# Moving the splits of the last output weight and of the adapter weights, and the making of the expert masks, forward in a one-core decoder layer

## The chip, the cores and the metric

The kernel runs on one core of one Trainium2 chip. The metric is the device time of one execution in microseconds (us): 538.18 us before the change, the median of 3 runs (537.94 to 539.28). Engines are PE (matrix products), DVE (vector), ACT (scalar), POOL (GpSimd) and SP, which here issues all the transfers.

## The reference, cut to what matters

`x` is 2 x 256 rows of 512. The layer does three things, each with a layer norm in front and a residual sum behind:

```
x += attn(ln(x))        32 heads of 128; q, k normed over all 4096 columns; out @ Wo + bo
x += fq(ln(x)) @ fq(ctx)            fake quantisation to 256 levels on both sides
x += base(ln(x)) + lora(ln(x))      15 router logits, softmax, top 8, expert_map -> 8 gates
```

In the last part `h = ln(x) @ A.T` gives 8 experts x 16 columns, each expert's columns are multiplied by its gate, and the product with `B` is added. The gate of an expert is the sum of the kept router probabilities whose entry of `expert_map` is that expert.

## The kernel before, in words

Matrix products are made with a split: each f32 operand is written as a rounded part ("hi", fp32r) and the remainder ("lo", operand minus hi), and a product is hi*hi + hi*lo + lo*hi, three matmuls. ACT makes the hi parts (a copy), DVE or POOL the lo parts (a subtraction whose inputs are both in SBUF, for weights, k and q).

The first 190 us or so project k and q for all 32 heads. Then come 16 pairs of heads, `pair(p)` on every engine, p = 0 to 15; each pair has four slots j = 0 to 3, one for each head and batch row. Pairs 1 to 10 stand in a hardware loop, pairs 11 to 15 are written out, so that `peeled(p, first, end)` can put something into one of them alone. Pair 15 (`last=True`) has no v projection for a following pair and no fourth v or output weight.

The order on each engine is written by hand. In a slot PE does: scores of the next slot (`scores`, L529 to L542), transposes of this slot's probabilities (L544), a tile of the next pair's v (L552), output projection of the head before (`project_out`, L569), and probabilities times v (`probs_v`, L590). At even slots nothing new is needed for the scores; at odd slots `scores` begins with a new head, and waits for its k and q splits, `pe.wait_ge(kq_lo, 2 * h + 2)` at L533. These k_lo and q_lo are made by POOL at the start of the even slot (`split_kq_lo`, L951), from k_hi and q_hi of ACT (L748, L751). There is one buffer each. In every slot POOL also makes the lo part of one weight (`chunk_lo`, L942: w_lo at even slots, wo_lo at odd ones), behind ACT's hi part (L745, L827).

DVE in a slot: o_lo of the head before (L1200, even slots), the row maximum nmax of the scores (L1178), nbias = nmax * rq_t (L1180, a tiny product of two SBUF tensors for which ACT's exponentials wait, L762), pt_lo (L1247), the reciprocal rinv and two scalings of the probabilities by it (L1186, L1188, L1189; PE's transposes wait for these), and v_lo at odd slots (L1194).

The last output weight (head 31) has buffers of its own: it is loaded at L383 behind the loads of pair 14, its hi part is made by ACT in slot 0 of pair 15 (L820), its lo part by POOL in slot 2 (L986). The adapter weights ra (A and the router, 576 columns) and bm (B, 512 columns) are loaded at L372 and L373; ACT makes their hi parts behind pair 15 (L839, L841), POOL the lo parts in slot 3 of pair 15 (`split_low_rank`, L969). The expert masks (`mark_experts`, L960: a cast of the map and 8 comparisons of 128x15) are made by POOL in the quantisation stage behind the pairs (L1008). DVE reads them at L1386.

Of the kernel before, what the change touches and what calls it, by code (L numbers as in the profile page):

```python
# [19 lines left out]
F32 = mybir.dt.float32  # L20
# [3 lines left out]
ALU = mybir.AluOpType  # L24
# [3 lines left out]
P = 128  # L28
B, S, D = 2, 256, 512
# [4 lines left out]
NH, DH = 32, 128  # L34
NP = NH // 2
# [13 lines left out]
def decoder_layer(nc, x, ctx_t, wk, wq, wv, wo, bk, bq, bv, bo, gk, gq, qscal, ra_w, base_b, router_b, bm_w,  # L49
                  expert_map, out):  # L50
    st = ExitStack()
    with st:
# [20 lines left out]
        def here(name, shape, dt, at=None):  # L73
            return place(name, shape, dt, at)[0]
# [56 lines left out]
        KS = T * 4  # L131
# [39 lines left out]
        bm_lo = here("bm_lo", [P, D], F32R, q_at + 21 * KS)  # L171
        wo_last_hi = here("wo_last_hi", [P, D], F32R, q_at + 22 * KS)
        wo_last_lo = here("wo_last_lo", [P, D], F32R, q_at + 23 * KS)
        wo_last_f = here("wo_last_f", [P, D], F32, q_at + 26 * KS)
        o_last_hi = here("o_last_hi", [P, T], F32R, q_at + 24 * KS)
        o_last_lo = here("o_last_lo", [P, T], F32R, q_at + 25 * KS)
        hwt_hi = here("hwt_hi", [P, NT, P], F32R, qh_at)
# [106 lines left out]
        def peeled(n, first, end):  # L284

            return isinstance(n, int) and first <= n < end
# [22 lines left out]
        @block.sync  # L309
        def _(sp):  # L310
            for t in range(NT):
                sp.dma_start(xin[:, t, :], x[t]).then_inc(x_landed[t], 16)
            for r in range(4):
                sp.dma_start(raw[:, r, :], wk[r]).then_inc(w_landed[r], 16)
            for dst, src in ((bk_c, bk), (bq_c, bq), (bv_c, bv), (g_c, gk), (gq_c, gq)):
                sp.dma_start(dst[:], src).then_inc(const_landed, 16)

            def load_heads(w, i, before):

                for r in range(4):  # L320
                    sp.wait_ge(w_lo_dve, before + 4 * i + r - 3)
                    sp.dma_start(raw[:, r, :], w[bass.ds(4 * i + r, 1)].rearrange("a p n -> (a p) n")
                                 ).then_inc(w_landed[r], 16)

            sp.dma_start(qs_b[:], qscal.partition_broadcast(P)).then_inc(qs_landed, 16)
            for i in range(1, NH // 4):
                load_heads(wk, i, 0)
                if i <= NT:
                    g = slice(2 * (i - 1), 2 * i)
                    sp.dma_start(ctx_f[:, g, :], ctx_t[:, g, :]).then_inc(ctx_landed[i - 1], 16)  # L330
                if i == NT:
                    sp.dma_start(bo_b[:], bo.partition_broadcast(P)).then_inc(x_bo_landed, 16)
                    for t in range(NT):
                        sp.dma_start(xb[:, t, :], x[t]).then_inc(x_bo_landed, 16)
            sp.wait_ge(ctx_quantised, B * NC // 2)
            sp.dma_start(ctx_kept, ctx_k[:]).then_inc(ctx_kept_out, 16)
            with sp.Fori(0, NH // 4) as i:
                load_heads(wq, i, NH)

            def load_wv(pair, c, n):  # L340
                sp.dma_start(raw[:, n, :], wv[bass.ds(2 * pair + c, 1)].rearrange("a p n -> (a p) n")
                             ).then_inc(w_landed[n], 16)

            def load_wo(h):
                sp.dma_start(raw[:, 1, :], wo[bass.ds(h, 1)].rearrange("a p n -> (a p) n")
                             ).then_inc(w_landed[1], 16)

            for n in range(4):

                sp.wait_ge(w_lo_dve, U1 - 3 + n if n < 2 else U1 + n - 1)  # L350
                load_wv(n // 2, n % 2, n % 2)

            def pair_loads(p):
                for j in range(3 if peeled(p, NP - 1, NP) else 4):
                    if peeled(p, 0, 1) and j < 2:
                        sp.wait_ge(w_lo_dve, U1 + 3 + j)
                    else:
                        sp.wait_ge(w_lo_pool, 4 * p + j - 1)
                    if j % 2:
                        load_wo(2 * p + j // 2)  # L360
                    else:
                        load_wv(p + 2, j // 2, 0)

            pair_loads(0)
            with sp.Fori(1, 8) as p:
                pair_loads(p)

            pair_loads(8)
            pair_loads(9)
            sp.wait_ge(scores_ready, 2 * 18)  # L370
            pair_loads(10)
            sp.dma_start(ra_f[:], ra_w).then_inc(ra_landed, 16)  # L372
            sp.dma_start(bm_f[:], bm_w).then_inc(bm_landed, 16)  # L373
            sp.dma_start(bb_b[:], base_b.partition_broadcast(P)).then_inc(base_b_landed, 16)
            sp.dma_start(rb_b[:], router_b.partition_broadcast(P)).then_inc(router_b_landed, 16)
            sp.dma_start(em_i[:], expert_map.partition_broadcast(P)).then_inc(map_landed, 16)
            pair_loads(11)
            sp.wait_ge(scores_ready, 2 * 22)
            sp.wait_ge(ctx_kept_out, 16)
            sp.dma_start(ctx_q[:], ctx_kept).then_inc(ctx_back, 16)  # L380
            for p in range(12, NP - 1):
                pair_loads(p)
            sp.dma_start(wo_last_f[:], wo[NH - 1]).then_inc(wo_last_landed, 16)  # L383
            pair_loads(NP - 1)
            for t in range(NT):
                sp.wait_ge(out_done, t + 1)
                sp.dma_start(out[t], xn[:, t, :]).then_inc(stored, 16)
            sp.wait_ge(stored, 16 * NT)
# [297 lines left out]
        def _(act):  # L686
# [55 lines left out]
            def pair_weights_hi(n, buf, half_, landed):  # L742

                act.wait_ge(w_landed[n], 16 * (NH // 2 + landed))
                act.copy(w_hi[:, buf, half_ * 512:(half_ + 1) * 512], raw[:, n, :]).then_inc(w_hi_done, 1)  # L745
# [48 lines left out]
            def pair(p, par, last=False):  # L794
                for j in range(4):
# [19 lines left out]
                        exps(h + b, 1 - b)  # L815
                    if b == 1 and not last:
                        v_half_hi(p + 1, j // 2, 1 - par)
                    if last and j == 0:
                        act.wait_ge(wo_last_landed, 16)
                        act.copy(wo_last_hi[:], wo_last_f[:]).then_inc(wo_last_hi_done, 1)  # L820
                    if last and j == 3:
                        pass
                    elif b == 1:
                        act.wait_ge(w_landed[1], 16 * (NH // 2 + 3 + 2 * p + j // 2))
                        if not peeled(h, 0, 1):
                            act.wait_ge(wo_used, h)
                        act.copy(wo_hi[:], raw[:, 1, :]).then_inc(w_hi_done, 1)  # L827
                    else:
                        pair_weights_hi(0, par, j // 2, 3 + 2 * p + j // 2)

            pair(0, 0)
            with act.Fori(0, (NP - 6) // 2) as i:
# [2 lines left out]
            for p in range(NP - 5, NP - 1):  # L835
                pair(p, p % 2)
            pair(NP - 1, 1, last=True)
            act.wait_ge(ra_landed, 16)
            act.copy(ra_hi[:], ra_f[:]).then_inc(rab_hi_done, 1)  # L839
            act.wait_ge(bm_landed, 16)  # L840
            act.copy(bm_hi[:], bm_f[:]).then_inc(rab_hi_done, 1)  # L841
            last_out_hi(1)


# [60 lines left out]
        def _(pool):  # L905
# [41 lines left out]
            def pair_chunk_lo(buf, half_, slot, n):  # L947
                cols = slice(half_ * 512, (half_ + 1) * 512)
                chunk_lo(w_lo[:, buf, cols], w_hi[:, buf, cols], slot, n)
# [16 lines left out]
                    ins = pool.tensor_scalar(onehot[:, e, :], emf[:], float(e), None, ALU.is_equal)  # L966
                ins.then_inc(experts_marked, 1)

            def split_low_rank():  # L969

                pool.wait_ge(rab_hi_done, 1)
                pool.tensor_tensor(ra_lo[:], ra_f[:], ra_hi[:], ALU.subtract).then_inc(rab_lo_done, 1)
                pool.wait_ge(rab_hi_done, 2)
                pool.tensor_tensor(bm_lo[:], bm_f[:], bm_hi[:], ALU.subtract).then_inc(rab_lo_done, 1)

            def pair(p, par, last=False):
                for j in range(4):
                    h = 2 * p + j // 2
                    if j % 2 == 0 and not (last and j == 2):
                        split_kq_lo(h + 1)  # L980
                    if last and j == 3:
                        split_low_rank()
                        break
                    if last and j == 2:
                        pool.wait_ge(wo_last_hi_done, 1)
                        pool.tensor_tensor(wo_last_lo[:], wo_last_f[:], wo_last_hi[:], ALU.subtract  # L986
                                           ).then_inc(wo_last_done, 1)
                    if j % 2:
                        chunk_lo(wo_lo[:], wo_hi[:], 1, 4 + 4 * p + j)
                    else:  # L990
                        pair_chunk_lo(par, j // 2, 0, 4 + 4 * p + j)
                    if peeled(p, NP - 5, NP - 4) and j == 0:
                        pool.memset(ones_b[:], 1.0).then_inc(ones_b_made, 1)

# [9 lines left out]
            for g in range(2):  # L1004
                pool.wait_ge(var_ready, g + 1)
                pool.tensor_tensor(rstd[:, 2 * g:2 * g + 2], vare[:, 2 * g:2 * g + 2], mhalf[:, 0:2], ALU.pow
                                   ).then_inc(rstd_ready, 1)
            mark_experts()  # L1008
            for t in range(NT):
                pool.wait_ge(var_ready, 3 + t)  # L1010
                pool.tensor_tensor(rstd[:, t:t + 1], vare[:, t:t + 1], mhalf[:, 0:1], ALU.pow).then_inc(rstd_ready, 1)
# [448 lines left out]
```

## Time and profile before

| | us |
|---|---|
| median of 3 runs | 538.18 (537.94 to 539.28) |
| the profiled execution's own time | 540.05 |
| its span, first to last instruction | 537.7 |
| PE busy in the span | 523.5 |
| DVE, ACT, POOL busy | 331.1, 355.9, 271.6 |

All times in views are from the start of the span. The engines' busy times overlap. The granted TensorE clock is 1.00 all through. In the profiled execution the projections end near 190 us, pair 13 is the stretch from 441.35 to 460.10, pair 14 that to 478.87, pair 15 that to 496.30; the quantised product, the experts and the output follow to 537.7. Where a view lists an instruction, the first number is its start and the second its duration.

### The profile page before, as it was taken

How to read it: one execution, taken by the hardware profiler on the slowest of the kernel's cores; microseconds unless marked ns; L12 is line 12 of the kernel's file. 1: busy time of each engine (PE TensorE's matmuls, PEld its weight loads, DVE VectorE, ACT ScalarE, POOL GpSimd, SP SyncE). 2: the span in 40 equal slices, each digit the busy share in tenths (PEclk: the TensorE clock that was granted, in tenths of full speed). 3: DMA queues.
4: the chain of work that ended last, by engine and by line, in shares of the span. 5: the costliest groups of instructions: out<-in, count | busy, mean ns of one | idle time of the engine just before them, and what ended most of it. 6: DMA issues, size and time to landing. Idle time of an engine off the chain costs nothing.

```text
span 537.7 us, 9702 instructions
## 1 busy us (share of the span) xinstructions
PE 523.5 (97%) x3198; PEld 462.0 (86%) x3198; DVE 331.1 (62%) x695; ACT 355.9 (66%) x745; POOL 271.6 (51%) x229
## 2 busy tenths in 40 slices
PE   6999999999999999999999999999999999999887
PEld 6888888888888888999999999999999999986475
DVE  6254444266666677666666666666666666676755
ACT  3566666556666767777777677767767776775740
POOL 3344444365454445554646455464646556465340
PEclk9999999999999999999999999999999999999999
DMA  5344635323332221112122111211142311220002
GB/s 182 126 139 134 230 96 174 89 89 98 94 100 83 74 81 55 47 57 60 59 59 59 57 43 56 59 59 59 59 121 62 126 50 60 60 78 21 2 0 79
DMA packets 23350, 43.41 MB, mean 81 GB/s; under 512 B 3616, under 2 KB 3616, under 8 KB 23072
## 3 DMA queue, kind: packets, MB, share of 16 engines
q1 hardware_dynamic: 23328, 43.13, 26.3%
q8 instruction: 12, 0.20, 0.2%
q14 instruction: 10, 0.08, 0.0%
HBM read 41.03 MB, written 2.10 MB: 80 GB/s over the span
## 4 chain that ended last, share of the span: by engine, by line
PE 90%; DVE 5%; ACT 2%; DMA 1%; issue 1%; POOL 1%; SPq 0%; DVEq 0%
PE p_t L483 5%; PE p_v L562 5%; PE p_v L564 5%; PE p_o L483 5%; PE p_t L484 5%; PE p_o L484 5%; PE p_v L563 5%; PE p_o L486 5%; PE p_t L486 5%; PE acc L581 5%; PE acc L582 5%; PE acc L583 5%; PE p_t L548 5%; PE p_o L600 3%; PE p_o L602 3%; PE p_o L601 3%
## 5 line engine op out<-in xcount | busy, mean ns | idle before, releaser
L1078 DVE TENSOR_TENSOR w_lo<-raw,w_hi 128x512 fp32r<-128x512 f32 x64 | 44.2, 690 | 78.0 <-ACT w_hi L693 78.0
L945 POOL TENSOR_TENSOR wo_lo<-raw,wo_hi 128x512 fp32r<-128x512 f32 x31 | 40.1, 1294 | 100.4 <-ACT wo_hi L827 100.4
L693 ACT CAST w_hi<-raw 128x512 fp32r<-128x512 f32 x64 | 39.9, 623 | 67.5 <-PE p_t L486 30.3
L762 ACT ACTIVATE probs<-p_s,nbias,rq_t 128x256 f32<-128x256 f32 x128 | 71.3, 562 | 19.1 <-DVE nbias L1180 19.1
L562 PE MATMUL p_v<-w_hi,xnt_hi 128*128 128x256 f32 x256 | 77.2, 301 | 0.0
L564 PE MATMUL p_v<-w_hi,xnt_lo 128*128 128x256 f32 x256 | 72.3, 282 | 0.0
L563 PE MATMUL p_v<-w_lo,xnt_hi 128*128 128x256 f32 x256 | 72.2, 282 | 0.0
L927 POOL TENSOR_TENSOR acc_k<-acc_k,square 128x512 f32<-128x512 f32 x32 | 41.7, 1304 | 53.3 <-ACT square L708 53.3
L927 POOL TENSOR_TENSOR acc_q<-acc_q,square 128x512 f32<-128x512 f32 x32 | 43.5, 1361 | 40.2 <-ACT square L708 39.9
L811 ACT CAST pt_hi<-p_t 128x512 fp32r<-128x512 f32 x64 | 37.4, 584 | 38.8 <-PE p_t L548 38.8
L945 POOL TENSOR_TENSOR w_lo<-raw,w_hi 128x512 fp32r<-128x512 f32 x32 | 44.9, 1403 | 20.5 <-ACT w_hi L745 20.5
L1178 DVE TENSOR_REDUCE nmax<-p_s 128x2 f32<-128x512 f32 x64 | 43.9, 686 | 14.9 <-PE p_s L541 14.0
L483 PE MATMUL p_t<-xnt_hi,w_hi 128*128 128x512 f32 x128 | 50.4, 394 | 0.7 <-ACT xnt_hi L717 0.7
L581 PE MATMUL acc<-wo_hi,o_hi 128*128 128x512 f32 x124 | 49.4, 398 | 1.0 <-POOL wo_lo L945 0.6
L484 PE MATMUL p_t<-xnt_hi,w_lo 128*128 128x512 f32 x128 | 49.8, 389 | 0.0
L483 PE MATMUL p_o<-xnt_hi,w_hi 128*128 128x512 f32 x128 | 49.8, 389 | 0.0
L484 PE MATMUL p_o<-xnt_hi,w_lo 128*128 128x512 f32 x128 | 49.8, 389 | 0.0
L486 PE MATMUL p_o<-xnt_lo,w_hi 128*128 128x512 f32 x128 | 49.8, 389 | 0.0
L562 PEld LDWEIGHTS p_v<-w_hi,xnt_hi 128*128 128x128 f32 x256 | 48.8, 190 | 0.3 <-issue 0.2
L582 PE MATMUL acc<-wo_hi,o_lo 128*128 128x512 f32 x124 | 49.0, 395 | 0.0
L563 PEld LDWEIGHTS p_v<-w_lo,xnt_hi 128*128 128x128 f32 x256 | 48.9, 191 | 0.0
L564 PEld LDWEIGHTS p_v<-w_hi,xnt_lo 128*128 128x128 f32 x256 | 48.7, 190 | 0.0
(263 smaller groups left out, 1483.7 us busy)
## 6 DMA issues: line engine op xcount, KB each, us to landing
raw<-in_wv SPq DMA_DIRECT2D x36, 256.0 KB, 2.6
raw<-in_wk SPq DMA_DIRECT2D x32, 256.0 KB, 2.6
raw<-in_wq SPq DMA_DIRECT2D x32, 256.0 KB, 2.6
raw<-in_wo SPq DMA_DIRECT2D x31, 256.0 KB, 2.6
ctx_f<-in_ctx SPq DMA_DIRECT2D x4, 512.0 KB, 3.6
xin<-in_x SPq DMA_DIRECT2D x4, 256.0 KB, 3.5
xb<-in_x SPq DMA_DIRECT2D x4, 256.0 KB, 6.0
ctx_kept<-ctx_k SPq DMA_DIRECT2D x1, 1024.0 KB, 5.0
```

The lines of the kernel that those rows point to most:

```text
L483: pe.matmul(p_flat[2 + n], hi[:, c, :], xnt_hi[:, c, :], start=(c == 0), stop=False)
L484: pe.matmul(p_flat[2 + n], lo[:, c, :], xnt_hi[:, c, :], start=False, stop=False)
L486: mm = pe.matmul(p_flat[2 + n], hi[:, c, :], xnt_lo[:, c, :], start=False, stop=(c == NC - 1))
L562: pe.matmul(p_v[:, t % 2, :], xnt_hi[:, c, tt], hi[:, c, :], start=(c == 0), stop=False)
L563: pe.matmul(p_v[:, t % 2, :], xnt_hi[:, c, tt], lo[:, c, :], start=False, stop=False)
L564: mm = pe.matmul(p_v[:, t % 2, :], xnt_lo[:, c, tt], hi[:, c, :], start=False, stop=(c == NC - 1))
L581: pe.matmul(acc[t][:], oh[:, tt], wh[:], start=False, stop=False, skip_group_check=True)
L582: pe.matmul(acc[t][:], ol[:, tt], wh[:], start=False, stop=False, skip_group_check=True)
L762: act.activation(probs[:, b, a, :], p_s[:, a, :], ACT.Exp, bias=nbias[:, b, a:a + 1], scale=rq_t[:, 2 * b + a:2 * b + a + 1], accum_out=rs ...
L927: pool.tensor_tensor(sums[:], sums[:], square[:, r % 2, :], ALU.add).then_inc(summed, 1)
L945: pool.tensor_tensor(dst, raw[:, slot, :], hi, ALU.subtract).then_inc(w_lo_pool, 1)
L1078: dve.tensor_tensor(w_lo[:, n, 0:NC * DH], raw[:, r, :], w_hi[:, n, 0:NC * DH], ALU.subtract).then_inc(w_lo_dve, 1)
```

## The change

Four things move, nothing is computed otherwise:

- The transfer of the last output weight is issued by SP right behind that of bm, before pair 11's loads (it stood behind pair 14's); its buffer lies over head 4 of k_all, which is dead by then.
- ACT makes ra_hi in slot 0 of pair 13, bm_hi in slot 1 and wo_last_hi in slot 2, each behind the hi part of that slot's weight.
- POOL makes ra_lo, bm_lo and wo_last_lo in the same slots, each behind the lo part of that slot's weight.
- POOL makes the expert masks at the end of slot 3 of pair 14.

```
-        wo_last_f = here("wo_last_f", [P, D], F32, q_at + 26 * KS)
+        wo_last_f = here("wo_last_f", [P, D], F32, k_at + 4 * KS)
 # SP
             sp.dma_start(bm_f[:], bm_w).then_inc(bm_landed, 16)
+            sp.dma_start(wo_last_f[:], wo[NH - 1]).then_inc(wo_last_landed, 16)
...
                 pair_loads(p)
-            sp.dma_start(wo_last_f[:], wo[NH - 1]).then_inc(wo_last_landed, 16)
             pair_loads(NP - 1)
 # ACT, in pair()
-                    if last and j == 0:
-                        act.wait_ge(wo_last_landed, 16)
-                        act.copy(wo_last_hi[:], wo_last_f[:]).then_inc(wo_last_hi_done, 1)
...
+                    if peeled(p, NP - 3, NP - 2):
+                        if j == 0:
+                            act.wait_ge(ra_landed, 16)
+                            act.copy(ra_hi[:], ra_f[:]).then_inc(rab_hi_done, 1)
+                        elif j == 1:
+                            act.wait_ge(bm_landed, 16)
+                            act.copy(bm_hi[:], bm_f[:]).then_inc(rab_hi_done, 1)
+                        elif j == 2:
+                            act.wait_ge(wo_last_landed, 16)
+                            act.copy(wo_last_hi[:], wo_last_f[:]).then_inc(wo_last_hi_done, 1)
...
             pair(NP - 1, 1, last=True)
-            act.wait_ge(ra_landed, 16)
-            act.copy(ra_hi[:], ra_f[:]).then_inc(rab_hi_done, 1)
-            act.wait_ge(bm_landed, 16)
-            act.copy(bm_hi[:], bm_f[:]).then_inc(rab_hi_done, 1)
 # POOL; last_weights_lo(j) holds the three subtractions, one for each j = 0, 1, 2
                     if last and j == 3:
-                        split_low_rank()
                         break
-                    if last and j == 2:
-                        pool.wait_ge(wo_last_hi_done, 1)
-                        pool.tensor_tensor(wo_last_lo[:], wo_last_f[:], wo_last_hi[:], ALU.subtract
-                                           ).then_inc(wo_last_done, 1)
                     if j % 2:
                         chunk_lo(wo_lo[:], wo_hi[:], 1, 4 + 4 * p + j)
                     else:
                         pair_chunk_lo(par, j // 2, 0, 4 + 4 * p + j)
+                    if peeled(p, NP - 3, NP - 2):
+                        last_weights_lo(j)
+                    if peeled(p, NP - 2, NP - 1) and j == 3:
+                        mark_experts()
...
-            mark_experts()
             for t in range(NT):
                 pool.wait_ge(var_ready, 3 + t)
```

## Rows read from the trace of the kernel before

**Rows 1.** The page's engine line: busy us, share of the span, instructions.
```profile
PE 523.5 (97%) x3198; PEld 462.0 (86%) x3198; DVE 331.1 (62%) x695; ACT 355.9 (66%) x745; POOL 271.6 (51%) x229
```

**Rows 2.** Windows, pairs 13 and 15: length; busy PE, PEld, DVE, ACT, POOL; clock; DMA.
```profile
441.35:460.10 18.75, 18.75 (x138) 17.72 (x137) 12.56 (x28) 13.62 (x33) 10.49 (x8) 1.00 0.19 57
...
478.87:496.30 17.43, 15.42 (x90) 11.97 (x88) 10.97 (x23) 12.47 (x29) 11.45 (x9) 1.00 0.09 31
```

**Rows 3.** Timeline of PE in slot 3 of pair 13: start, duration, instruction.
```profile
455.43 0.28 PE L539 MATMUL p_s<-k_hi,q_hi 128*128 128x256 f32 x1
...
456.15 0.60 PE L548 MATMUL p_t<-ident,probs 128*128 128x128 f32 x4
```

**Rows 4.** Timeline of POOL in slots 0 to 2 of pair 13; idle before, its releaser in brackets.
```profile
446.11 1.41 POOL L945 TENSOR_TENSOR w_lo<-raw,w_hi 128x512 fp32r<-128x512 f32 x1 [0.58 <-ACT w_hi L745]
450.97 1.29 POOL L945 TENSOR_TENSOR wo_lo<-raw,wo_hi 128x512 fp32r<-128x512 f32 x1 [3.46 <-ACT wo_hi L827]
452.35 1.30 POOL L953 TENSOR_TENSOR k_lo<-k_all,k_hi 128x512 fp32r<-128x512 f32 x1
453.61 1.30 POOL L955 TENSOR_TENSOR q_lo<-q_all,q_hi 128x512 fp32r<-128x512 f32 x1
455.49 1.41 POOL L945 TENSOR_TENSOR w_lo<-raw,w_hi 128x512 fp32r<-128x512 f32 x1 [0.58 <-ACT w_hi L745]
```

**Rows 5.** Timeline of DVE in pair 13.
```profile
447.70 0.16 DVE L1180 TENSOR_TENSOR nbias<-nmax,rq_t 128x2 f32<-128x2 f32 x1
...
455.14 0.36 DVE L1188 TENSOR_SCALAR probs<-probs,rinv 128x256 f32<-128x256 f32 x1
455.40 0.35 DVE L1189 TENSOR_SCALAR probs<-probs,rinv 128x256 f32<-128x256 f32 x1
```

**Rows 6.** Timeline of ACT in pair 13, slots 0 and 1.
```profile
447.40 0.59 ACT L811 CAST pt_hi<-p_t 128x512 fp32r<-128x512 f32 x1 [1.38 <-PE p_t L548]
...
450.27 0.62 ACT L827 CAST wo_hi<-raw 128x512 fp32r<-128x512 f32 x1 [0.70 <-PE acc L583]
```

**Rows 7.** The low part of ra on POOL: duration ns min/median/max, starts.
```profile
L972 POOL TENSOR_TENSOR ra_lo<-ra_f,ra_hi x1: 1427/1427/1427, 494.0 to 494.0; 128x576 fp32r<-128x576 f32 x1
```

**Rows 8.** DVE's scaling L1163 near 110 us, all four instances: ns min/median/max.
```profile
L1163 DVE TENSOR_SCALAR diag<-ident,rk_t x4: 276/793/1316, 109.6 to 112.3; 128x128 f32<-128x128 f32 x4
```

**Rows 9.** Timeline of POOL beside them.
```profile
109.57 2.72 POOL L927 TENSOR_TENSOR acc_q<-acc_q,square 128x512 f32<-128x512 f32 x2
```

**Rows 10.** Timeline of POOL, the expert masks.
```profile
501.99 0.21 POOL L963 CAST emf<-em_i 128x15 f32<-128x15 int32 x1
502.29 2.24 POOL L966 TENSOR_SCALAR onehot<-emf 128x15 f32<-128x15 f32 x8
```

**Rows 11.** Timeline of POOL across the start of pair 15 and its slot 2.
```profile
479.11 1.28 POOL L945 TENSOR_TENSOR wo_lo<-raw,wo_hi 128x512 fp32r<-128x512 f32 x1 [3.46 <-ACT wo_hi L827]
480.49 1.30 POOL L953 TENSOR_TENSOR k_lo<-k_all,k_hi 128x512 fp32r<-128x512 f32 x1
481.74 1.28 POOL L955 TENSOR_TENSOR q_lo<-q_all,q_hi 128x512 fp32r<-128x512 f32 x1
...
488.63 1.29 POOL L986 TENSOR_TENSOR wo_last_lo<-wo_last_f,wo_last_hi 128x512 fp32r<-128x512 f32 x1
```

**Rows 12.** Timeline of PE in pair 15: the scores of head 31, and the last transposes.
```profile
483.33 0.28 PE L539 MATMUL p_s<-k_hi,q_hi 128*128 128x256 f32 x1
...
492.08 0.66 PE L548 MATMUL p_t<-ident,probs 128*128 128x128 f32 x4 [0.51 <-DVE probs L1189]
```

**Rows 13.** Timeline of DVE in pair 15: nbias in slots 0 and 2.
```profile
481.18 0.62 DVE L1180 TENSOR_TENSOR nbias<-nmax,rq_t 128x2 f32<-128x2 f32 x1
...
489.24 0.70 DVE L1180 TENSOR_TENSOR nbias<-nmax,rq_t 128x2 f32<-128x2 f32 x1
```

**Rows 14.** Timeline of SP's transfers after the three small ones.
```profile
398.28 0.43 SPq L376 DMA_DIRECT2D em_i<-in_em  x1
400.81 0.33 SPq L341 DMA_DIRECT2D raw<-in_wv  x1
```

More of the change, by code:

```diff
@@ L967, in mark_experts, with last_weights_lo @@
                 ins.then_inc(experts_marked, 1)
[L969 to L974, printed above, removed]
+            def last_weights_lo(j):
+                if j == 0:
+                    pool.wait_ge(rab_hi_done, 1)
+                    pool.tensor_tensor(ra_lo[:], ra_f[:], ra_hi[:], ALU.subtract).then_inc(rab_lo_done, 1)
+                elif j == 1:
+                    pool.wait_ge(rab_hi_done, 2)
+                    pool.tensor_tensor(bm_lo[:], bm_f[:], bm_hi[:], ALU.subtract).then_inc(rab_lo_done, 1)
+                elif j == 2:
+                    pool.wait_ge(wo_last_hi_done, 1)
+                    pool.tensor_tensor(wo_last_lo[:], wo_last_f[:], wo_last_hi[:], ALU.subtract
+                                       ).then_inc(wo_last_done, 1)
             def pair(p, par, last=False):
```

## Prediction, made before the changed kernel ran

> **What bounds the kernel now.** I read the page's engine line first: PE is busy 97% of the span [rows 1]. Then the windows by pair: in pair 13 PE is busy 18.75 of 18.75 us while POOL has 10.49 us of work and ACT 13.62; in pair 15 PE has 15.42 of 17.43 us and the others are no fuller [rows 2]. So up to the end of pair 14 whatever makes PE wait is paid in full, since PE has no later idle time there to give it back, and work taken off ACT, DVE or POOL gains nothing. In pair 15 and behind it the end is set by chains through all engines. The third view is the timeline of each engine in pairs 13 and 15, which shows what has room. Times below are those of before, with delays added.
>
> POOL sits idle 3.46 us ahead of wo_lo, but almost nothing lies between wo_lo, k_lo and q_lo, and q_lo ends at 453.61 + 1.30 = 454.91 [rows 4], when PE wants to begin the scores of the new head at 455.43 [rows 3]. That is 0.52 us of room. In pair 15 q_lo ends at 481.74 + 1.28 = 483.02 and the scores begin at 483.33 [rows 11, 12]: 0.31 us. The question is what is put in front of these two.
>
> **A lock between DVE and POOL.** nbias is a product of 128x2. It takes 0.16 us in an odd slot, when POOL is idle [rows 5], and 0.70 us at 489.24 [rows 13], and that one ends at 489.94, just when POOL's wo_last_lo ends (488.63 + 1.29 = 489.92) [rows 11]. The one at 481.18 ends at 481.80, with k_lo (481.79). So a small DVE operation with both inputs in SBUF waits for POOL's whole subtraction. The DVE scaling L1163, one SBUF tensor by a column of scalars like L1188 and L1189, takes 276 ns at its shortest and 1316 at its longest, with a median of 793 [rows 8], while POOL runs two additions back to back in 2.72 us [rows 9]. Two short and two long ones fit only if the first waited for the first addition, POOL's second addition then got in ahead of DVE's second scaling, and that waited once more. I take that as the rule for L1188 and L1189: under back-to-back POOL work each of the two can wait for one POOL operation.
>
> The Trainium skill ("SBUF — State Buffer", "Who interferes with whom") says of the same thing that a DVE instruction with two SBUF inputs contends with a GpSimd instruction that reads SBUF, and that a tensor_scalar contends if it is in a 2-port mode; the loser blocks for the whole instruction. The nbias rows agree with its first half. Were L1188 and L1189 not in such a mode, the sum would lose the handover term below.
>
> **SP's transfer.** One issue more near 397 us. The last small one starts at 398.28 and the next weight load at 400.81, waiting for POOL [rows 14], so 0.43 us more is hidden in 2.1 us; if it weren't, that load would start 0.4 us late and still be long ahead of its use. The removed issue at pair 14 gains nothing. Cost 0 (bounds 0 and 0.4).
>
> **ACT in pair 13.** ra_hi goes into 1.38 us of idle before pt_hi [rows 6]: free. wo_last_hi, in slot 2, goes into the like gap: free. bm_hi (a copy of the size of wo_hi, 0.62 [rows 6]) stands behind wo_hi with o_hi, k_hi, q_hi, pt_hi queued behind it; they slip by its 0.6 us, but POOL, busy with bm_lo, takes k_hi and q_hi later still, and o_lo, which follows o_hi, stays ahead of PE's product. So nothing is added to what follows; if that cover failed, 0.2 us.
>
> **POOL in pair 13, slot 0.** ra_lo (1.43) [rows 7] starts when w_lo ends, 446.11 + 1.41 = 447.52, and ends at 448.95. nbias starts at 447.70 and has both inputs in SBUF [rows 5], so it ends at 448.95 and not at 447.86: 1.09 us late. The exponentials follow it. PE needs the result two microseconds later, so PE loses nothing here, but ACT is late: of the 1.1 us, wo_hi has 0.70 of idle ahead of it [rows 6] and starts 0.35 late.
>
> **POOL in pair 13, slots 1 and 2.** wo_lo starts at 450.97 + 0.35 = 451.32. Back to back, one POOL subtraction starts 1.25 us after the other (453.61 less 452.35 [rows 4]). So bm_lo starts at 452.57, k_lo at 453.82, q_lo at 455.07, and q_lo ends at 456.37. With 0.1 us for the signal PE starts the scores at 456.5 and not at 455.43 [rows 3]: 1.05 us late. The bounds of this part: 1.25 less 0.52 = 0.7 (bm_lo alone, no delay from slot 0), and 1.2.
>
> Then the handover. L1188 starts at 455.14, L1189 at 455.40, both just after q_lo's end in the trace before [rows 4, 5]. Now they come while q_lo runs to 456.37. L1188 waits for it; w_lo is queued on POOL by then, gets in next, and runs for 1.25 us to about 457.7; L1189 ends near 457.9. PE's transposes need it. They started at 456.15 [rows 3] and start now at 457.9: 1.8 us late. This holds the 1.05 within it, so the handover adds 0.75. The bounds of the handover are 0 and 0.9. From then on all engines run 1.8 us late in the same order, and wo_last_lo, put behind w_lo, has POOL's idle 3.46 us as cover; nbias of slot 3 waits for it until 459.0, but the exponentials behind it also stand behind pt_hi, and that behind the transposes of 457.9, so it costs nothing more.
>
> **POOL at the end of pair 14.** The masks take from 501.99 to 504.53, 2.54 us for nine instructions [rows 10]. They start behind wo_lo at 479.11 + 1.28 = 480.39 (again in the clock of before). k_lo started at 480.49 [rows 11], so k_lo and q_lo start 2.4 us later and q_lo ends at about 485.4. In the same stretch L1188 and L1189 of slot 0 fall on k_lo and q_lo and hand the lock over twice, 0.1 each: 485.6. PE starts the scores of head 31 at 485.75 in place of 483.33 [rows 12]: 2.4 us. Bounds: 2.1 (no handover) and 2.7.
>
> What comes back of it: nbias in slot 2 took 0.70 us because of wo_last_lo [rows 11, 13], which is gone from there, and nothing else of POOL runs then, since wo_lo is ahead of it and w_lo waits for ACT's copy behind the exponentials. 0.70 less 0.16 is 0.54, and it lies on the chain nbias, exponentials, scalings, last transposes at 492.08 [rows 12]. The 0.46 us of slot 0 (0.62 less 0.16) is swallowed by the wait for the scores, and slot 1 follows PE. So pair 15 costs 2.4 less 0.54, some 1.85 us (bounds 1.3, if more of the nbias relief counts, and 2.3, if none does).
>
> **Behind the pairs.** ra_hi, bm_hi, ra_lo and bm_lo leave the end of pair 15, and the masks the quantisation stage. The last products there start when PE is ready, not when these are; POOL's next work, rstd, waits for DVE's variances. I cost their removal at 0 (bounds 0 and a gain of 0.1).
>
> **Sum.** 1.8 + 1.85 = 3.65 us later. Against the profiled execution's own time that is 540.05 + 3.65 = 543.7 us (span 541.3). That execution is 1.87 us above the median of the runs, so for a median I add the 3.65 to 538.18: 541.8 us. By the skill's condition failing (no 2-port mode for L1188 and L1189), it would be 541.0.
>
> **Rivals.**
>
> No handover: the scalings are not held by POOL, or DVE's second goes ahead of w_lo. Pair 13 costs 1.05 and pair 15 1.65: 2.7 us, 540.9. For it: L1188 and L1189 overlap with a running POOL operation nowhere in this trace, so the reading by L1163 is by likeness only. Against it: 1316 ns of L1163.
>
> The masks are cheaper: POOL takes them in without the 2.5 us, as the eight tiny comparisons overlap with the waits around them. Then pair 15 gains its 0.54, pair 13 costs 1.8: 1.3 us slower, 539.5, no change that can be told. Against it: k_lo follows wo_lo after 0.10 us; there is no wait to hide in.
>
> Not slower: the lock's relief decides. If q_lo of the new head reaches PE in time in both places (POOL's spans being rough, the 0.52 and 0.31 us of room would have to be 1.3 and 2.5), then the three nbias of pair 15 shorten, by 0.46 and 0.54 and that of slot 1 by as much at most, 1.5 us in all, and the time is 536.7 to 538.2. It decides from the point where the masks and bm_lo cost less than the room ahead of the scores. Against it: the POOL rows of pairs 13 and 15 agree with the ends of nbias to 0.02 us, so they are not rough by 0.8.
>
> Worse: the lag in pair 13 spills over. v_lo of slot 1 and o_lo of slot 2 come out of the delay of 1.1 us with some tenths left; if PE has to wait for one of them, or a further scaling loses the lock for 1.25 us, it is 3.65 and about 1: 542.8.
>
> **Chances.** Forecast 0.53, no handover 0.23, cheap masks 0.09, not slower 0.08, worse 0.07. About 0.3% (1.6 us) is what a measurement of this kernel can tell from no change. Slower by more than that: 0.83, the forecast, no handover and worse. Within: 0.13, the cheap masks and half of the not slower. Faster: 0.04. The range takes the low bounds 0.7 + 1.3 = 2.0 on one side, with 0.5 for the spread of the medians, and the high ones, 2.1 + 2.3 = 4.4, with 0.3 on the other: 539.7 to 542.9.
>
> **What would show it.** In the changed profile: q_lo in slot 2 of pair 13 ends over 1 us later against PE's slot than before, and PE is idle 1 us before L539; L1189 there lasts over 1 us and PE waits for it at L548; nbias in slot 0 lasts 1.2 us; the masks lie between wo_lo and k_lo, and PE waits over 2 us at L539 of head 31; nbias in slot 2 of pair 15 lasts 0.16. The stage behind pair 15 is as long as before. The prediction is wrong if PE shows no idle at these two L539, or if the nbias waits do not move with POOL's work.

## The result, and the profile after

The changed kernel takes 543.05 us (median of 11 runs, 541.61 to 545.02). The kernel before took 539.25 us in its 11 (537.94 to 541.50). The ratio is 1.0068, with a 95% interval of 1.0053 to 1.0083: slower by 3.7 us, 2.9 to 4.5. The forecast was 3.65 us slower and the rule behind it held, but the time of 541.8 stood on a median of 538.18 from three runs, and the range ended at 542.9. The measured 543.05 lies 0.15 us outside it. Ratios and intervals here are of runs in the fast state: one run of e2 (1287.98 us) and one of e9 (745.44 us) below were in the slow one, and only the medians of the table count them.

All stage times below are measured in one trace each, on PE, from the first scores (L539) of pair 13 to the last transposes of pair 15 (L548). That leaves out the start of the program, which differs from one execution to the next: pair 13 begins at 441.35 us in the trace of before, at 440.68 in that of after, and between 439.48 and 443.72 in all the traces here. From the last transposes to the end of the span it is 45.62 us before and 45.56 after.

| stage | before | after | difference | predicted |
|---|---|---|---|---|
| pair 13 | 18.76 | 20.41 | +1.65 | +1.8 |
| pair 14 | 18.76 | 18.76 | 0 | 0 |
| pair 15 to its last transposes | 13.21 | 14.99 | +1.78 | +1.85 |
| sum | 50.73 | 54.16 | +3.43 | +3.65 |

The window of pair 13 after, which answers to the first of [rows 2] (18.75 us, all of it busy), has 1.2 us without PE, and 14.22 us of POOL where there were 10.49:

```profile
440.68:461.09 20.41, 19.24 (x138) 17.78 (x137) 15.15 (x28) 15.03 (x36) 14.22 (x11) 1.00 0.19 52
```

PE's timeline after (start, duration, idle before and its releaser) has three new waits, the first three of these rows, that answer to [rows 3] and [rows 12]; the fourth was there before, with 0.51:

```profile
455.62 0.39 PE L539 MATMUL p_s<-k_hi,q_hi 128*128 128x256 f32 x1 [0.70 <-POOL q_lo L958]
457.07 0.66 PE L548 MATMUL p_t<-ident,probs 128*128 128x128 f32 x4 [0.47 <-DVE probs L1196]
...
486.58 0.39 PE L539 MATMUL p_s<-k_hi,q_hi 128*128 128x256 f32 x1 [2.37 <-POOL q_lo L958]
...
494.84 0.66 PE L548 MATMUL p_t<-ident,probs 128*128 128x128 f32 x4 [0.50 <-DVE probs L1196]
```

The two waits of pair 13 list 1.17 us of idle and the pair is 1.65 longer. That fits how PE's records lie: in a stream of 128x256 matmuls each is 0.28 us long and starts 0.12 behind the one before, so that a stream that stops loses more than the idle listed.

POOL's timeline after, the same stretch as [rows 4], has ra_lo and then, from wo_lo on, six subtractions without a gap:

```profile
446.80 1.42 POOL L976 TENSOR_TENSOR ra_lo<-ra_f,ra_hi 128x576 fp32r<-128x576 f32 x1
450.56 1.28 POOL L948 TENSOR_TENSOR wo_lo<-raw,wo_hi 128x512 fp32r<-128x512 f32 x1 [2.33 <-ACT wo_hi L824]
451.80 1.28 POOL L979 TENSOR_TENSOR bm_lo<-bm_f,bm_hi 128x512 fp32r<-128x512 f32 x1
453.05 1.28 POOL L956 TENSOR_TENSOR k_lo<-k_all,k_hi 128x512 fp32r<-128x512 f32 x1
454.30 1.27 POOL L958 TENSOR_TENSOR q_lo<-q_all,q_hi 128x512 fp32r<-128x512 f32 x1
455.54 1.32 POOL L948 TENSOR_TENSOR w_lo<-raw,w_hi 128x512 fp32r<-128x512 f32 x1
456.82 1.32 POOL L982 TENSOR_TENSOR wo_last_lo<-wo_last_f,wo_last_hi 128x512 fp32r<-128x512 f32 x1
```

and DVE's timeline after has, where [rows 5] had 0.16, 0.36 and 0.35 us:

```profile
447.02 1.22 DVE L1187 TENSOR_TENSOR nbias<-nmax,rq_t 128x2 f32<-128x2 f32 x1
...
453.00 0.16 DVE L1187 TENSOR_TENSOR nbias<-nmax,rq_t 128x2 f32<-128x2 f32 x1
...
454.64 1.08 DVE L1195 TENSOR_SCALAR probs<-probs,rinv 128x256 f32<-128x256 f32 x1
455.64 1.37 DVE L1196 TENSOR_SCALAR probs<-probs,rinv 128x256 f32<-128x256 f32 x1
...
484.06 1.35 DVE L1196 TENSOR_SCALAR probs<-probs,rinv 128x256 f32<-128x256 f32 x1
...
492.54 0.16 DVE L1187 TENSOR_TENSOR nbias<-nmax,rq_t 128x2 f32<-128x2 f32 x1
```

The first scaling ends at 455.72, 0.15 us after q_lo (455.57). The second starts at 455.64 and ends at 457.01, 0.15 us after w_lo (456.86), which had started on POOL 0.10 us earlier. PE's transposes follow at 457.07. That is the handover. The nbias at 453.00 shows that it isn't so for every request: it comes as bm_lo gives way to k_lo and takes 0.16, although POOL has no gap there. DVE's operations that take one of their inputs from PSUM are no slower beside POOL: pt_lo takes 0.69 us beside k_lo (at 453.13), as it did with POOL idle before (at 448.03). So it isn't a general slowing of DVE. The last row is the relief: 0.16 where [rows 13] had 0.70.

At the start of pair 15 POOL has, where in [rows 11] k_lo followed wo_lo by 0.10 us:

```profile
480.09 1.28 POOL L948 TENSOR_TENSOR wo_lo<-raw,wo_hi 128x512 fp32r<-128x512 f32 x1 [3.46 <-ACT wo_hi L824]
481.32 0.20 POOL L966 CAST emf<-em_i 128x15 f32<-128x15 int32 x1
481.61 2.18 POOL L969 TENSOR_SCALAR onehot<-emf 128x15 f32<-128x15 f32 x8
483.87 1.39 POOL L956 TENSOR_TENSOR k_lo<-k_all,k_hi 128x512 fp32r<-128x512 f32 x1
485.22 1.30 POOL L958 TENSOR_TENSOR q_lo<-q_all,q_hi 128x512 fp32r<-128x512 f32 x1
```

### The profile page after: what moved, and what is told of

It reads as the page before. It is cut to its first block, busy times and chain, and to the rows that moved or that the text cites. A ratio compares the mean times of both kernels' runs of the same rounds, so it can differ in the third digit from the quotient of the medians.

```text
span 540.4 us, 9700 instructions
## 1 busy us (share of the span) xinstructions
PE 522.6 (97%) x3196; PEld 460.6 (85%) x3198; DVE 333.8 (62%) x695; ACT 355.6 (66%) x745; POOL 271.1 (50%) x229
## 4 chain that ended last, share of the span: by engine, by line
PE 88%; DVE 5%; ACT 3%; POOL 2%; DMA 1%; issue 1%; SPq 0%; DVEq 0%; ACTq 0%
PE p_t L483 5%; PE p_o L486 5%; PE p_o L483 5%; PE p_t L484 5%; PE p_o L484 5%; PE p_v L562 5%; PE p_v L564 5%; PE p_t L486 5%; PE p_v L563 5%; PE acc L581 5%; PE acc L582 5%; PE acc L583 5%; PE p_t L548 5%; PE p_o L600 3%; PE p_s L539 3%; PE p_s L541 3%
```

## The experiments

The columns are the median of the runs, the difference to the kernel before with its 95% interval (the ratio, turned into us by 539), and pair 13, the part of pair 15 and the whole stage in the one trace that each kernel has.

| kernel | median, us | against before, us | pair 13 | pair 15 part | stage |
|---|---|---|---|---|---|
| before | 538.8 to 539.25 | | 18.76 | 13.21 | 50.73 |
| changed | 543.05 | +3.7 (2.9 to 4.5) | 20.41 | 14.99 | 54.16 |
| e1 masks only | 541.72 | +2.6 (1.5 to 3.7) | 18.76 | 16.61 | 54.13 |
| e2 masks back | 540.13 | +0.5 (-0.5 to 1.5) | 20.44 | 12.60 | 51.80 |
| e3 output weight only | 538.47 | -0.7 (-1.7 to 0.2) | 18.76 | 12.62 | 50.14 |
| e4 even slots | 538.63 | -0.6 (-1.4 to 0.1) | 18.76 | 12.62 | 50.14 |
| e5 one scaling | 542.45 | +2.9 (1.6 to 4.0) | 19.73 | 16.31 | 54.81 |
| e6 three masks | 540.85 | +1.4 (0.3 to 2.5) | 18.76 | 14.21 | 51.73 |
| e7 bm alone in slot 1 | 539.87 | +0.5 (-0.4 to 1.4) | 20.18 | 12.61 | 51.55 |
| e8 masks, filled | 541.47 | +2.2 (1.5 to 3.0) | 18.76 | 15.33 | 52.85 |
| e9 changed, filled | 542.57 | +4.0 (2.7 to 5.3) | 20.41 | 15.03 | 54.21 |
| e10 changed again | 542.64 | +3.3 (2.4 to 4.4) | 20.44 | 16.19 | 55.39 |

My theory: the loss is POOL's work in front of k_lo and q_lo, in two places, with the handover of the lock behind each; the gain is the shorter nbias. Rivals: the masks alone, the splits alone, or that any additional work in these pairs costs PE.

**e1, masks only.** The kernel before with `mark_experts()` at the end of slot 3 of pair 14 and nothing else moved.

```
+                    if peeled(p, NP - 2, NP - 1) and j == 3:
+                        mark_experts()
...
-            mark_experts()
```

> Only the expert masks move to slot 3 of pair 14; the weight splits stay where they were. If the masks cost what they push k_lo and q_lo back (my theory), PE waits about 2.3 us for q_lo at the scores of head 31, and since wo_last_lo stays in slot 2 of pair 15 its nbias still lasts 0.5 us or more, unless the shift by 2.3 us takes wo_last_lo out of its way: +1.8 to +2.3 us against before. If the masks hide in POOL's idle time (rival), 0.

PE waits 2.39 us for q_lo, as predicted, but pair 15 takes 3.40 us more and not 1.8 to 2.3. The nbias of slot 2 lasts 0.47 us. The rest is a thing that no theory had, the clock. Windows of e1, 3 us up to the end of PE's wait and 5 us from there (length; busy time of PE, PEld, DVE, ACT, POOL; granted clock; DMA):

```profile
481.30:484.30 3.00, 0.61 (x7) 0.41 (x5) 1.77 (x3) 0.98 (x2) 2.92 (x4) 1.00 0.02 6
484.30:489.30 5.00, 5.00 (x23) 4.47 (x24) 2.33 (x6) 2.23 (x6) 1.17 (x1) 0.66 0.22 56
```

A mean of 0.66 over 5 us is 3.4 us at the lower of the two levels, 1.2 GHz (5 x 0.34 / 0.5). In it a 128x512 matmul of the output projection takes 0.63 us; in pair 14 of the same trace it takes 0.40.

**e2, masks back.** The changed kernel with the masks at their old place.

```
-                    if peeled(p, NP - 2, NP - 1) and j == 3:
-                        mark_experts()
```

> The changed kernel with the masks back behind the pairs. Theory: pair 13 costs its 1.6 us (PE idle 0.7 us at the scores of head 28 and 0.5 us at the transposes behind), and the nbias of slots 1 and 2 of pair 15 shorten to 0.16 us and give back about 0.8: +0.8 to +1.1 us against before. If the whole loss came from the masks, it is 0 or faster by 0.5.

Pair 13 costs 1.68, pair 15 gives back 0.61: +1.07 in the stage, as expected. The run times say +0.5 with an interval that holds it. So the masks were not the whole of the loss.

**e3, the output weight only.** The transfer, the buffer and both halves of the split in slot 2 of pair 13; ra, bm and the masks as before.

```
+                    if peeled(p, NP - 3, NP - 2) and j == 2:
+                        act.wait_ge(wo_last_landed, 16)
+                        act.copy(wo_last_hi[:], wo_last_f[:]).then_inc(wo_last_hi_done, 1)
```

> Only the last output weight moves (transfer, buffer, ACT's copy and POOL's subtraction in slot 2 of pair 13). Theory: slot 2 has POOL idle behind it, so pair 13 costs nothing; in pair 15 nbias of slot 1 shortens from 0.47 and that of slot 2 from 0.70 to 0.16 us: 0.5 to 0.85 us faster than before. If the lock between DVE and POOL is not what lengthens nbias, 0.

Pair 13 stays at 18.76 and the pair 15 part is 0.59 shorter. The run times, 0.7 faster with an interval that just holds zero, don't prove it. DVE's nbias in slots 1 and 2 of pair 15:

```profile
483.61 0.16 DVE L1186 TENSOR_TENSOR nbias<-nmax,rq_t 128x2 f32<-128x2 f32 x1
487.81 0.16 DVE L1186 TENSOR_TENSOR nbias<-nmax,rq_t 128x2 f32<-128x2 f32 x1
```

The earlier transfer and the new buffer cost nothing that can be seen. Of the runs with a mean clock of 0.999 or more the 8 of e3 have a median span of 535.75 us, the 23 of the kernel before 536.5.

**e4, even slots.** All four moved, each behind the w_lo of an even slot, where POOL then has 3.5 us of idle.

```
+                    if peeled(p, NP - 3, NP - 2) and j % 2 == 0:
+                        last_weights_lo(j // 2)
+                    if peeled(p, NP - 2, NP - 1) and j == 0:
+                        last_weights_lo(2)
+                    if peeled(p, NP - 2, NP - 1) and j == 2:
+                        mark_experts()
```

> All four moved, but each behind the w_lo of an even slot: ra in slot 0 and bm in slot 2 of pair 13, the last output weight in slot 0 of pair 14, the masks in slot 2 of pair 14. Theory: all of it falls into POOL's idle 3.5 us, k_lo and q_lo are in time, and pair 15 gains as in the kernel with the output weight alone: 0.5 to 0.85 us faster than before. Rival (any extra work in these pairs costs PE): 1 us or more slower.

Pairs 13 and 14 stay at 18.76 although nbias lasts 1.22 us in three of their slots: not any additional work costs, only that in front of k_lo and q_lo. The nbias at 477.88, beside the cast of the masks, takes 0.16. The same masks here, in POOL's timeline of pair 14:

```profile
476.41 1.41 POOL L947 TENSOR_TENSOR w_lo<-raw,w_hi 128x512 fp32r<-128x512 f32 x1 [0.58 <-ACT w_hi L745]
477.77 0.20 POOL L965 CAST emf<-em_i 128x15 f32<-128x15 int32 x1
478.05 2.25 POOL L968 TENSOR_SCALAR onehot<-emf 128x15 f32<-128x15 f32 x8
481.17 1.29 POOL L947 TENSOR_TENSOR wo_lo<-raw,wo_hi 128x512 fp32r<-128x512 f32 x1 [0.87 <-ACT wo_hi L824]
```

**e5, one scaling.** The changed kernel; in slot 2 of pair 13 one DVE product for both halves.

```
+                if once:
+                    dve.tensor_tensor(probs[:, b, :, :], probs[:, b, :, :],
+                                      rinv[:, b, :].unsqueeze(2).to_broadcast([P, 2, S]), ALU.mult
+                                      ).then_inc(p_normed, 1)
+                    return
```

> The changed kernel, with the two scalings of slot 2 of pair 13 made by one DVE product of both halves with the broadcast reciprocals, so that DVE asks for the lock once there. Theory: it waits for q_lo's end like the first scaling did, but w_lo can't get in between, so PE no longer waits at the transposes of head 28: the 0.5 us of idle goes, the wait for q_lo (0.7) stays, and pair 13 takes 19.6 us and not 20.4. If the transposes were late for another reason, pair 13 stays at 20.4.

Pair 13 takes 19.73 (20.41 without it), the wait at the transposes is gone, and now w_lo is the one that waits for DVE:

```profile
453.88 1.28 POOL L958 TENSOR_TENSOR q_lo<-q_all,q_hi 128x512 fp32r<-128x512 f32 x1
455.11 1.73 POOL L948 TENSOR_TENSOR w_lo<-raw,w_hi 128x512 fp32r<-128x512 f32 x1
```

```profile
454.21 1.50 DVE L1196 TENSOR_TENSOR probs<-probs,rinv 128x512 f32<-128x512 f32 x1
```

The handover is worth 0.68 us of the 1.65. The profiled execution as a whole was not faster, since its clock fell in pair 15 as in e1 (0.66 over the 5 us behind the wait of 2.37) and once more near 510 us. The three runs of e5 with a mean clock of 0.999 or more have a median span of 539.1, the six of the changed kernel 539.85; the intervals of the run times overlap.

**e6, three masks.** e1 with the cast and three comparisons in pair 14, the other five behind the pairs.

```
+                        mark_experts(0, 3)
...
+            mark_experts(3, NE)
```

> The kernel with the masks alone in pair 14, but only the cast and three of the eight comparisons there (the other five behind the pairs). Theory: what is in front of k_lo and q_lo is paid less the 0.3 us of room, so five comparisons of 0.28 us less make the wait for q_lo fall from 2.4 to about 1.0 us; and with a shorter idle of PE the clock stays at its higher level behind it: +0.3 to +1.0 us against before. If it is not the POOL time, the wait does not follow the number of comparisons.

The wait follows the number of comparisons, and is 0.63 us, less than the 1.0 expected: the comparisons take 1.48 us less (0.70 against 2.18), and DVE's scalings now come behind the start of k_lo, which lasts 1.29 us and not 1.40. But there is a second wait of 0.48 us at the transposes, the handover again, which with eight masks is hidden under the longer wait. DVE's scalings and PE:

```profile
482.85 1.16 DVE L1192 TENSOR_SCALAR probs<-probs,rinv 128x256 f32<-128x256 f32 x1
483.93 1.37 DVE L1193 TENSOR_SCALAR probs<-probs,rinv 128x256 f32<-128x256 f32 x1
```

```profile
483.91 0.39 PE L539 MATMUL p_s<-k_hi,q_hi 128*128 128x256 f32 x1 [0.63 <-POOL q_lo L955]
485.36 0.66 PE L548 MATMUL p_t<-ident,probs 128*128 128x128 f32 x4 [0.48 <-DVE probs L1193]
```

The stage is 1.00 longer, at the upper edge of what was expected. The run times say 1.4, with an interval of 0.3 to 2.5. Among the runs with a mean clock of 0.999 or more four have a span of 537.5 or 537.6, 1.0 to 1.1 over the 536.5 of the kernel before; the other five have up to 539.7. In the trace, one of these five (538.8), pair 13 begins at 441.40, and in that of e1 at 440.02; what makes the start of the program longer stays open.

**e7, bm alone.** As e4, but bm in slot 1 of pair 13 and ra in slot 2 of pair 12.

```
-                    if peeled(p, NP - 3, NP - 2) and j == 2:
+                    if peeled(p, NP - 3, NP - 2) and j == 1:
                         act.wait_ge(bm_landed, 16)
```

> As the kernel with everything behind even slots, but bm behind wo_lo in slot 1 of pair 13, and ra a pair earlier. Theory: one subtraction in front of k_lo and q_lo, with no delay of wo_hi by ra_lo, makes PE wait 0.6 to 0.8 us at the scores of head 28, and the handover of the lock adds 0.6 to 0.8 behind it: pair 13 takes 20.0 to 20.3 us against 18.76. If ra_lo or wo_last_lo were the cause, 18.76.

Pair 13 takes 20.18, within the 20.0 to 20.3 expected; 0.48 us of PE's idle is at the scores and 0.46 at the transposes, each less than the 0.6 to 0.8 expected. So one subtraction of 1.25 us in front of k_lo and q_lo costs 1.42 us, more than itself. The other 0.23 us of the changed kernel fit ra_lo's delay of wo_hi, which is not there in e7.

**e8, masks, filled.** e1 with nine useless matmuls in front of the scores of head 31.

```
+                    if last and j == 1:
+                        for n in range(FILL):
+                            pe.matmul(p_flat[0], ident_r[:], xnt_hi[:, 0, :], start=True, stop=True)
```

> The kernel with the masks alone in pair 14, and nine matmuls without use (128x512, about 2.1 us) on PE in front of the scores of head 31, so that PE is busy while it waits for q_lo. In that kernel the granted clock fell to half for 3.4 us right behind the 2.4 us of idle, and nine of its ten runs had a mean clock under 0.999. If the idle is what lowers the clock, most runs now have 0.999 or more and the time is about 1.7 us shorter than with the masks alone, near +1.3 to +1.9 against before. If the fall has nothing to do with the idle, the clock and the time are as with the masks alone, +2.6.

```profile
485.05:488.05 3.00, 2.63 (x15) 1.92 (x13) 1.75 (x3) 0.92 (x2) 2.92 (x4) 1.00 0.02 5
488.05:493.05 5.00, 4.92 (x32) 4.07 (x32) 2.79 (x7) 2.93 (x8) 2.46 (x2) 1.00 0.14 52
```

The wait that is left is 0.36 us. The clock stays at 1.00 behind it and the part of pair 15 takes 15.33 where e1 had 16.61. That is 2.12 more than before, within the 1.8 to 2.3 expected of the masks alone. Five of 8 runs had a mean clock of 0.999 or more, against one of 10 in e1. But a mean doesn't say where the clock fell: the profiled run of e8 has 0.994, and its fall lies between 10 and 20 us (0.66), far from this wait. Of 26 runs of the kernel before, made beside e8, 7 were under 0.999 too. The median time fell by 0.25 us only, with intervals that overlap (2.2 against 2.6 over the kernel before), and the median span from 539.95 to 538.8, while that of the kernel before beside them went from 536.9 to 536.55. The 1.7 us expected are not there.

**e9 and e10, the changed kernel filled and again.**

> The changed kernel with the nine matmuls without use in front of the scores of head 31. Theory: the late q_lo costs the same, so from the start of pair 13 to the last transposes it takes 54.1 to 54.3 us as before the filling, and the mean clock is 0.999 or more in more of the runs than in the changed kernel without them, with a median lower by up to 1 us. If the lower clocks of the changed kernel come from elsewhere in the program, the share of runs under 0.999 and the median stay.

> The changed kernel as it is, on the same chip as the filled one, for the comparison: +3.4 us against before where the clock stays up, more in runs in which it falls behind PE's wait of 2.4 us; 5 of its first 11 runs had a mean clock under 0.999.

e10 is the changed kernel, and in this execution its clock fell, in PE's window behind the wait of 2.37 us:

```profile
485.00:490.00 5.00, 4.59 (x20) 4.22 (x21) 1.83 (x5) 1.89 (x6) 1.59 (x2) 0.66 0.25 56
```

Its part of pair 15 took 16.19 and not 14.99. So the same program has both. e9's stage is 54.21, as expected, with the clock at 1.00 in it. In e10 three of 6 runs were under 0.999, in e9 one of the five that count, and the medians are alike (542.64, 542.57): the gain of up to 1 us is not there. Whether filling the wait shortens the changed kernel stays open.

## Why the prediction came out as it did

- **What bounds it**: right. No wait of PE up to the end of pair 14 was given back: pair 14 takes 18.76 in both traces, and the part behind the last transposes is as long as before.
- **The lock and its handover**: right. nbias of slot 0 lasts 1.22 us; the two scalings take 1.08 and 1.37 us, each to the end of one POOL subtraction; e5 takes 0.68 us away with one request for the lock in place of two. The Trainium skill ("SBUF — State Buffer", "Who interferes with whom") lets a tensor_scalar contend only in a 2-port mode; by these rows the two scalings do contend. The rule was right, but two readings under it were not. In the rows of L1163 it was not the second scaling that waited: the trace has 1.31 us from 109.64, 0.28 from 110.87, 1.32 from 111.06 and 0.28 from 112.30, so the second got through between POOL's two additions and the third waited. And the rival without handover was given in its favour that the two scalings overlap with POOL nowhere. They do: L1189 runs from 455.40 to 455.75 and w_lo starts at 455.49 [rows 4, 5]. In the trace of before w_lo lasts 1.40 us or more in the 31 slots of the pairs where it starts during a scaling, and 1.29 in the one where it doesn't. That POOL waits for DVE could have been read there. The same rival's time stands as 540.9 in one place and as 541.0 in another, since the second keeps the two handovers of pair 15.
- **Pair 13**: 1.65 us where 1.8 was forecast. The scores came 0.86 us late and not 1.05. The term that was too large is the start of the chain: ACT's wo_hi (449.85 after) began 0.24 us late, so POOL's wo_lo began 0.26 us late (450.56 and the shift of 0.67 between the traces, against 450.97 [rows 4]) and not 0.35, and the signal to PE took 0.05 us and not 0.1. The transposes came 1.59 us late (457.07 and the shift, against 456.15 [rows 3]), so the handover added 0.73 where 0.75 was forecast; the last 0.06 of the 1.65 came behind them.
- **The masks**: right in mechanism. The scores came 2.27 us late (486.58 less 479.85, against 4.46 before) where 2.4 was forecast, and 0.49 of the 0.54 us of relief came back: 1.78 against 1.85. Of the two scalings of slot 0 only the second waited, to the end of k_lo (the row at 484.06), and not one on k_lo and one on q_lo.
- **Costed at nothing** (transfer, ACT's copies, work gone from behind the pairs): e3 and e4 agree; pairs 13 and 14 are unchanged in them. The weight load behind the additional transfer starts at 400.14, which is the 400.81 of [rows 14] less the shift of 0.67, and the part behind the last transposes is 0.06 us shorter.
- **Missed**: the granted clock. PE's wait of 2.4 us is followed in some executions by 3.4 us at 1.2 GHz, 1.2 to 1.3 us of time (e10 against the first trace, e1 against e8). I had costed an idle PE at its own length only. The clock fell there in three of the four traces with this wait (e1, e5, e10) and in none of the eight without it; that is why I take the wait for the cause, though e4, e5 and e8 show falls at other places too. Of the 17 runs of the changed kernel 8 had a mean clock under 0.999. The six of the first 11 at or above it have a median span of 539.85, against 536.5 for the 23 such runs of the kernel before that ran beside e1 to e4: 3.35 us, the stage's 3.43 again. What the medians show above that (3.8) can be the clock; that its falls in those runs were in pair 15 is not shown. So it is in part luck that the measured difference lies as near to 3.65: the stage alone gave 3.43, and the clock, which had no term, can have made up the rest.
- **The step that failed** is "for a median I add the 3.65 to 538.18", with 0.3 us above the high bounds for the spread. The base was the term of the sum that was too small: the median of three runs was 1.07 us below that of eleven, 539.25, and that is most of the 1.25 us by which 541.8 missed 543.05. The profiled execution of before, at 540.05, lay 1.87 above it, which was a warning of how far single executions spread. Added to 539.25 the forecast is 542.9.

## What to carry to other kernels

Idle time of a helper engine is not one pool: look for the next operation behind the place where work is inserted, and who waits for it last. POOL was half idle here, and the same masks cost nothing behind w_lo and 2.3 us in front of k_lo. Where POOL's work runs back to back, a DVE operation that needs the shared lock can pay up to one whole POOL operation, unless it comes just as POOL changes over, so count requests for the lock and not their length. And when a change is worth a few tenths of a per cent, a median of three runs can be further off than the sum: here 1.07 us against 0.22.

## What the runs showed that I had not expected

The granted clock went down to 1.2 GHz for 3.4 us behind a single wait of PE of 2.4 us, in a stretch of 3 us in which it was busy for 0.6; the same program did so in one profiled execution and not in another (0.66 against 1.00 over 5 us). In none of the traces with shorter waits, 0.4 to 0.7 us, did it fall in these pairs. The two kernels that gain in the stage, e3 and e4, are 0.59 us shorter there than the kernel before; by run times they are 0.6 to 0.7 us faster, with intervals that reach zero, and by the median spans of the runs with a mean clock of 0.999 or more 0.75 and 0.5 us.
